# Low half of an expert's first weight matrix, moved from VectorE to GpSimd in a fused attention, FFN and mixture-of-experts kernel

## The chip, the cores and the metric

The kernel runs on one core of one Trainium2 chip. The metric is the device time of one execution in microseconds (us). A core has five engines that work at the same time and meet at semaphores: TensorE (PE: matrix products), VectorE (DVE), ScalarE (ACT), GpSimd (POOL) and SyncE (SP, which here only issues DMA transfers). Each takes its own instructions strictly in the order of the program.

## The reference

Four blocks act in turn on x of shape 16 x 128 x 256, each with a residual: cross attention with 16 heads; a gated FFN with fake quantisation; an mLSTM-like attention with 4 heads; and a mixture of 8 experts, of which every token uses 2. The change touches only the last:

```
logits = einsum('btd,de->bte', x, gate_w)
expert_weights, expert_indices = top_k(softmax(logits), 2)
expert_weights = expert_weights / expert_weights.sum(-1, keepdims=True)
for i in range(8):
    wi = where(expert_indices == i, expert_weights, 0).sum(-1)
    h = silu(x @ w1[i]) * (x @ w3[i])
    out = out + (h @ w2[i]) * wi[..., None]
```

w1 and w3 are 256 x 1024 for each expert, w2 is 1024 x 256.

## The kernel before, in words

The part around the change has two stages.

**Routing (about 357 to 385 us of the profiled execution).** VectorE works through one long chain of small instructions, lines 1820 to 1917. It picks each token's two experts (lines 1831 to 1842), counts the tokens of each expert (1849, 1850), lays the (token, expert) pairs into 39 tiles of 128 rows, all tiles of one expert side by side (1853 to 1887), and builds one-hot matrices (1891 to 1897) out of which TensorE makes the token number of every row (1033). `link_d` puts a wait behind nearly every one of these, so that each starts when the one before it has ended. Three results leave the chain. `tile_info` (lines 1870 to 1872, released by `info_ready` at 1874) holds the expert, the buffer and a flag "new expert" for each tile. The four one-hot pieces of line 1897 release TensorE's products of line 1033. `row_token` (line 1917, `info_ready` again) is what GpSimd needs for its gathers.

**Tiles (from about 385 us to the end).** For each of 39 tiles GpSimd gathers 128 token rows (`gather_rows`, line 667), TensorE transposes them (1059), ScalarE makes the bf16 high half of the transposed rows (`x_high`, 1333) and VectorE the low half (`x_low`, 1952); then come the products with w1 and w3 (`gate_up_half`, 1052), SiLU and product (1329, 1931), the transposes of the result (1065), its halves (1337, 1956), the product with w2 (1074), the weighting (1948) and the scatter-add by GpSimd (675).

All products of the experts are done as three bf16 products: high x high, high x low, low x high. So each weight matrix is stored twice, as a bf16 high half and a bf16 low half, which is the matrix minus its high half. `expert_w` has room for three experts; in it the high half of matrix n (0 is w1, 1 is w3, 2 is w2) is at n * PART and the low half at (3 + n) * PART. PART is 2048 elements in each of 128 partitions.

**The first expert** is known before the routing is, and is treated apart. SyncE loads its three matrices to `first_w` (line 463). ScalarE makes the high halves with `first_high` (1318): of matrices 0 and 1 before the pair weights, at 356.79 us for 3.70 us, of matrix 2 behind them. VectorE makes the low halves with `first_low` (lines 1919 to 1922): `first_low(0)` and `first_low(1)` behind `row_token` (1924, 1925), then, behind `x_low(0, 0)`, `first_low(2)` (1976). Who waits for these: TensorE for `part_low[0]` and `part_low[1]` before its first products of tile 0 (1050) and for `part_low[2]` before its first product with w2 (1070); ScalarE for all three at lines 1374 and 1375; SyncE for each before it loads that matrix for tile 2 (479).

**Later experts** are loaded to `stage`, and their halves made by `weights_high` on ScalarE (1346), by GpSimd for matrix 0 (`weights_low`, line 694) and by VectorE for matrices 1 and 2 (line 1911), only where the flag says that the tile has a new expert.

**GpSimd's order in the routing.** Constants (630 to 646), a gather that only warms up the queue (649), five small instructions for the pair weights (653 to 660, the second a power), and then nothing until `row_token` is there (wait at 678): then the gathers of tile 0 and tile 1 (680, 682), the wait at 698 and the loop over the tiles. SyncE stores the routed rows (`xrow_dram`, line 470) when line 660 has ended.

**TensorE's order** is the products of line 1033 in four groups of eight, then 40 products with no use but to keep the engine's clock up (`keep_clock(40, 0)`, lines 1096 and 714), then the transposes of tile 0 (1097) and `tile_step` 0.

Of the kernel before, what the change touches and what calls it, by code (L numbers as in the profile page):

```python
# [8 lines left out]
def build(nc, x, ctx_in, wq, wkv, wout, clip_x, clip_down, w_gate, w_up, w_down, ig_k, ig_b, fg_k, fg_b, rms_scale,  # L9
# [6 lines left out]
    ALU = mybir.AluOpType  # L16
# [13 lines left out]
    IR = I0 - (IT - 1) * P  # L30
    QMAX = 127.0
    E, _, F1 = w1.shape
    FH = F1 // 2
    TOP = 2
# [3 lines left out]
    PART = KT * F1  # L38
# [22 lines left out]
    with stack:  # L61
# [6 lines left out]
        def sem(name):  # L68
            return stack.enter_context(nc.semaphore(name))
# [102 lines left out]
        down_out = (down_even, down_odd)  # L172
        hT, x1n, xq = lay(region2, (F32, IT, B * P), (F32, B, D), (BF16, KT, B * P))
        _, hq = lay(region2, (F32, IT, B * P), (BF16, IT, B * P))


# [27 lines left out]
        expert_w = region2[:, :].bitcast(BF16)  # L204
        first_w = region2[:, SLOT // 2:SLOT].rearrange("p (n c) -> p n c", c=PART)
# [153 lines left out]
        part_high = [sem(f"part_high{i}") for i in range(3)]  # L359
        part_low = [sem(f"part_low{i}") for i in range(3)]  # L360
# [148 lines left out]
        def _(pool):  # L509
# [148 lines left out]
            pool.wait_ge(pair_weights, 4)  # L658
            nc.gpsimd.tensor_tensor(xrow[:, :, D + 2], w12[:, 0, :], w12[:, 1, :], ALU.subtract).then_inc(xrow_routed, 1)
            nc.gpsimd.tensor_tensor(xrow[:, :, D + 3], e2, w12[:, 0, :], ALU.mult).then_inc(xrow_routed, 1)  # L660

            def gather_rows(t):

                if t >= 2:
                    pool.wait_ge(tx_done, t - 1)
                    pool.wait_ge(meta_ready, t - 1)
                pool.indirect_dma_start(xg[:, t % 2, :], None, xrow_dram,  # L667
                                        bass.IndirectOffsetOnAxis(ap=row_token[:, t:t + 1], axis=0)).then_inc(xg_loaded[t % 2], 16)
# [716 lines left out]
        def _(dve):  # L1385
# [533 lines left out]
            def first_low(n):  # L1919
                dve.wait_ge(part_high[n], 1)  # L1920
                tt(expert_w[:, (3 + n) * PART:(4 + n) * PART], first_w[:, n, :], expert_w[:, n * PART:(n + 1) * PART],
                   ALU.subtract).then_inc(part_low[n], 1)

            first_low(0)
            first_low(1)
            info = [None, tile_values(1)]

# [74 lines left out]
```

## Time and profile before

| | us |
|---|---|
| median of 3 runs | 757.08 |
| lowest and highest of the 3 | 752.0, 757.09 |
| profiled execution | 756.54 |
| its span, from first to last instruction | 754.8 |
| outside the span (756.54 - 754.8) | 1.74 |

The profile is of one execution. A group of rows names engine, source line and shape; "x2" behind a row means that two instructions were merged, and its time is that of both. "Busy" counts the time in which an instruction of the engine is under way, and that includes time in which it is held up.

### The profile page before, as it was taken

To read this page: it belongs to the slowest core of one execution; us is meant where nothing else is said; L and a number is where in the kernel's file an instruction comes from. 1 tells how busy PE (TensorE), PEld (TensorE's weight loads), DVE (VectorE), ACT (ScalarE), POOL (GpSimd) and SP (SyncE) were. 2 spreads that over 40 slices of the span, in tenths; PEclk is the share of its full clock that TensorE was granted. 3 is DMA by queue.
4 is the path that set the end of the run, shared out by engine and by line. 5 is a ranking of instruction groups with operands and counts; after the bars stand their busy time and mean duration, and the time that the engine had idled before them with its cause. 6 is when DMAs were issued, how large, how long until landed. Compare 5 with 4: busy or idle time off the path is not lost.

```text
span 754.8 us, 17035 instructions
## 1 busy us (share of the span) xinstructions
PE 657.7 (87%) x4890; PEld 464.8 (62%) x4890; DVE 500.0 (66%) x1180; ACT 375.3 (50%) x878; POOL 291.9 (39%) x358
## 2 busy tenths in 40 slices
PE   2799999997777776898099999999999999999992
PEld 2588888886534545786056666666666666666661
DVE  6389899998588967797954746555464747554430
ACT  1366666665686643786223535363543635543320
POOL 3111111121153625577233736464553637543321
PEclk9799999999999999699589999999999999999996
DMA  8200000000300005336405253533415264421114
GB/s 282 47 15 14 14 14 14 14 0 1 112 0 1 0 1 172 128 82 226 135 23 174 49 150 76 150 85 84 140 31 153 73 181 126 116 43 29 31 15 125
DMA packets 47414, 59.01 MB, mean 78 GB/s; under 512 B 13328, under 2 KB 41168, under 8 KB 47056
## 3 DMA queue, kind: packets, MB, share of 16 engines
q1 hardware_dynamic: 39808, 47.72, 19.5%
q0 software_dynamic: 7536, 10.44, 7.8%
q8 instruction: 34, 0.56, 0.3%
q14 instruction: 36, 0.29, 0.1%
HBM read 145.96 MB, written 11.73 MB: 209 GB/s over the span
## 4 chain that ended last, share of the span: by engine, by line
PE 58%; DVE 20%; issue 8%; ACT 5%; DMA 2%; POOL 2%; DVEq 2%; ACTq 1%; SPq 0%; POOLq 0%
PE psum L1052 19%; PE psum L1074 11%; PE psum L752 5%; PE psum L1065 4%; PE psum L736 3%; PE psum L759 3%; PE psum L772 2%; ACT region L1346 2%; PE psum L791 1%; PE psum L741 1%; PE psum L714 1%; DVE region L1759 1%; DVE region L1777 1%; PE psum L779 1%; DVE region L1956 1%
## 5 line engine op out<-in xcount | busy, mean ns | idle before, releaser
L1052 PE MATMUL psum<-region 128*128 (+1 forms) x936 | 214.8, 379 | 1.6 <-DVE region L1952 1.6
L1052 PEld LDWEIGHTS psum<-region 128*128 128x128 bf16 x936 | 91.5, 98 | 95.5 <-DVE region L1952 1.2
L1329 ACT ACTIVATE region<-psum 128x512 f32<-128x512 f32 x78 | 46.5, 597 | 179.6 <-PE psum L1052 178.7
L675 POOL DMA_INDIRECT sum_dram<-region,row_token x39 | 75.2, 1927 | 135.3 <-DVE region L1948 135.3
L1074 PE MATMUL psum<-region 128*128 (+1 forms) x936 | 110.5, 275 | 5.3 <-DVE region L1956 5.3
L1074 PEld LDWEIGHTS psum<-region 128*128 128x128 bf16 x936 | 91.4, 99 | 18.9 <-issue 7.5
L1931 DVE TENSOR_TENSOR region<-psum,region 128x512 f32<-128x512 f32 x78 | 53.8, 690 | 68.3 <-ACT region L1329 68.3
L545 POOL TENSOR_TENSOR region<-region,pair_mask 128x256 f32<-128x256 f32 x32 | 21.3, 687 | 128.3 <-ACT region L1114 128.3
L1956 DVE TENSOR_TENSOR region<-psum,region 128x1024 bf16<-128x1024 f32 x39 | 47.6, 1221 | 17.7 <-ACT region L1337 17.5
L667 POOL DMA_INDIRECT region<-xrow_dram,row_token x39 | 41.4, 1062 | 38.0 <-DVE row_token L1917 13.6
L1421 DVE TENSOR_REDUCE region<-psum 128x8 f32<-128x1024 f32 x32 | 39.0, 1218 | 18.4 <-PE psum L752 18.4
L1948 DVE TENSOR_SCALAR region<-psum,region 128x256 f32<-128x256 f32 x39 | 18.8, 482 | 43.2 <-PE psum L1074 43.2
L1337 ACT ACTIVATE region<-psum 128x1024 bf16<-128x1024 f32 x39 | 39.9, 1023 | 13.4 <-PE psum L1065 13.4
L752 PE MATMUL psum<-region 32*128 32x256 f32 x256 | 38.1, 417 | 3.7 <-POOL region L545 3.6
L1118 ACT ACTIVATE region<-region 128x1024 f32<-128x1024 f32 x32 | 33.8, 1058 | 14.5 <-DVE region L1423 14.5
L1065 PEld LDWEIGHTS psum<-ident,region 128*128 128x128 f32 x312 | 36.5, 141 | 7.3
L714 PE MATMUL psum<-ident_b 128*128 128x256 bf16 x308 | 40.8, 288 | 0.0
L1065 PE MATMUL psum<-ident,region 128*128 128x128 f32 x312 | 40.4, 273 | 0.0
L1346 ACT ACTIVATE region<-region 128x2048 f32 x21 | 40.1, 1907 | 0.0
L1423 DVE TENSOR_TENSOR region<-psum,region 128x1024 f32<-128x1024 f32 x32 | 39.2, 1224 | 1.1
L1911 DVE TENSOR_TENSOR region<-region 128x2048 f32 x14 | 38.6, 2755 | 1.3 <-issue 1.3
L736 PE MATMUL psum<-region 128*128 128x128 f32 x256 | 34.4, 292 | 3.6 <-DMA region<-in_L_xattn_Wout 3.6
(298 smaller groups left out, 1220.3 us busy)
## 6 DMA issues: line engine op xcount, KB each, us to landing
region<-in_L_ffn_w SPq DMA_DIRECT2D x117, 1024.0 KB
region<-in_ctx SPq DMA_DIRECT2D x32, 128.0 KB, 2.4
xrow_dram<-region SPq DMA_DIRECT2D x1, 2080.0 KB, 7.8
x_sb<-in_x SPq DMA_DIRECT2D x4, 512.0 KB, 8.0
region<-in_ctx SPq DMA_DIRECT2D x2, 1024.0 KB, 7.0
region<-neg_max_dram SPq DMA_DIRECT2D x1, 2048.0 KB, 11.5
sum_dram<-x_sb SPq DMA_DIRECT2D x1, 2048.0 KB, 7.5
region<-neg_max_dram SPq DMA_DIRECT2D x4, 256.0 KB, 4.0
```

The lines of the kernel that those rows point to most:

```text
L667: pool.indirect_dma_start(xg[:, t % 2, :], None, xrow_dram, bass.IndirectOffsetOnAxis(ap=row_token[:, t:t + 1], axis=0)).then_inc(xg_loade ...
L675: pool.indirect_dma_start(sum_dram, bass.IndirectOffsetOnAxis(ap=row_token[:, t:t + 1], axis=0), y_d[:, t % 2, :], None, compute_op=ALU.ad ...
L714: mm(psum[:, bank_no, 0:256], ident_b[:], ident_b[:].unsqueeze(1).to_broadcast([P, 2, P]), start=True, stop=True)
L736: last = mm(bank1[:, m, :], w, xcT[:, p, (m // KT) * KT + k, :], start=(k == 0), stop=(k == KT - 1))
L752: last = mm(S_ps[s][:, 4 * r + 2 * m:4 * r + 2 * m + 2, :], qkT[rows, p, m, :], kbd[rows, p, m, :, :], start=True, stop=True)
L1052: last = mm(psum[:, 2 * f + n, :], (xT_lo if xl else xT_hi)[:, p, k, :], weights_at(place, wl, n, k * F1 + f * FH, FH), start=(i == 0), st ...
L1065: last = tr(bank(4, F1 // P, P, count=2)[:, f, :], h_d[:, p, f * P:(f + 1) * P], ident[:])
L1074: last = mm(psum[:, 7, 0:D], (hT_lo if hl else hT_hi)[:, f, :], weights_at(place, wl, 2, f * D, D), start=(i == 0), stop=(i == 3 * (F1 // ...
L1329: act_fn(sil_d[:, f, :], psum[:, 2 * f, :], ACT.Silu).then_inc(sil_d_ready, 1)
L1346: act_fn(expert_w[:, bass.ds(place + n * PART, PART)], stage[:, p, n, :], ACT.Copy)
L1931: tt(h_d[:, p, f * FH:(f + 1) * FH], psum[:, 2 * f + 1, :], sil_d[:, f, :], ALU.mult).then_inc(h_d_ready, 1)
L1956: tt(hT_lo, bank(4, F1 // P, P, count=2), hT_hi, ALU.subtract).then_inc(hT_low, 1)
```

## The change

GpSimd gets one instruction behind its pair weights: it waits for the high half of matrix 0 of the first expert, and subtracts it from that matrix. VectorE's call of `first_low(0)` behind `row_token` goes. Nothing else changes; the function `first_low` stays for matrices 1 and 2.

```diff
             nc.gpsimd.tensor_tensor(xrow[:, :, D + 2], w12[:, 0, :], w12[:, 1, :], ALU.subtract).then_inc(xrow_routed, 1)
             nc.gpsimd.tensor_tensor(xrow[:, :, D + 3], e2, w12[:, 0, :], ALU.mult).then_inc(xrow_routed, 1)
 
+            pool.wait_ge(part_high[0], 1)
+            nc.gpsimd.tensor_tensor(expert_w[:, 3 * PART:4 * PART], first_w[:, 0, :], expert_w[:, 0:PART], ALU.subtract).then_inc(part_low[0], 1)
+
             def gather_rows(t):
...
-            first_low(0)
             first_low(1)
             info = [None, tile_values(1)]
```

## Rows read from the trace of the kernel before

**Rows 1.** The page of the profile: busy shares (part 1) and the chain (part 4).
```profile
...
PE 657.7 (87%) x4890; PEld 464.8 (62%) x4890; DVE 500.0 (66%) x1180; ACT 375.3 (50%) x878; POOL 291.9 (39%) x358
...
PE 58%; DVE 20%; issue 8%; ACT 5%; DMA 2%; POOL 2%; DVEq 2%; ACTq 1%; SPq 0%; POOLq 0%
...
```

**Rows 2.** Chain that ended last, 350 to 430 us (start us, us, what).
```profile
...
373.02 4.55 DVE x_q L1897 x4
...
378.06 6.68 PE psum L714 x40
384.74 0.23 PE psum L1059 x2
385.00 0.39 ACT region L1333
...
385.83 2.21 DVE region L1921
...
```

**Rows 3.** Timeline of VectorE, 353 to 400 us; in brackets idle time and its releaser.
```profile
...
363.02 0.48 DVE L1858 TENSOR_TENSOR region<-region 128x312 f32<-128x312 f32 x1
...
365.43 0.20 DVE L1868 TENSOR_TENSOR region<-region 128x39 f32<-128x39 f32 x1
...
366.38 0.16 DVE L1875 TENSOR_TENSOR region<-region 128x8 f32<-128x8 f32 x1
...
378.39 0.20 DVE L1917 SCALAR_TENSOR_TENSOR row_token<-psum,row_empty 128x39 uint32<-128x39 f32 x1
378.51 4.48 DVE L1921 TENSOR_TENSOR region<-region 128x2048 bf16<-128x2048 f32 x2
385.41 0.42 DVE L1952 TENSOR_TENSOR region<-psum,region 128x256 bf16<-128x256 f32 x1 [2.42 <-ACT region L1333]
...
```

**Rows 4.** Timeline of GpSimd, 353 to 760 us.
```profile
...
361.56 2.94 POOL L655 TENSOR_TENSOR region<-region,minus_one 128x16 f32<-128x16 f32 x1
...
365.06 0.23 POOL L660 TENSOR_TENSOR region<-region 128x16 f32<-128x16 f32 x1
378.88 2.83 POOL L667 DMA_INDIRECT region<-xrow_dram,row_token  x1 [13.59 <-DVE row_token L1917]
382.02 1.81 POOL L667 DMA_INDIRECT region<-xrow_dram,row_token  x1 [0.30 <-issue]
...
416.93 3.81 POOL L694 TENSOR_TENSOR region<-region 128x2048 f32 x1
...
```

**Rows 5.** Line 667, the gathers: durations in ns, min/median/max, and to landing.
```profile
...
L667 POOL DMA_INDIRECT region<-xrow_dram,row_token x39: 940/997/2835, 378.9 to 710.6; - x39
...
DMA to landing us min/median/max: 2.6/2.9/5.5
```

**Rows 6.** SyncE's DMA queue, 360 to 400 us: waited in total, times, longest.
```profile
...
SPq L481 <- DVE region L1921: 10.0, 3, 5.7
...
```

**Rows 7.** Timeline of ScalarE, 353 to 400 us.
```profile
...
356.79 3.70 ACT L1318 ACTIVATE region<-region 128x2048 bf16<-128x2048 f32 x2
...
```

**Rows 8.** Timeline of VectorE, 412 to 432 us.
```profile
...
417.15 0.69 DVE L1931 TENSOR_TENSOR region<-psum,region 128x512 f32<-128x512 f32 x1 [1.31 <-ACT region L1329]
...
419.67 3.21 DVE L1911 TENSOR_TENSOR region<-region 128x2048 f32 x1 [0.18 <-issue]
...
428.88 2.29 DVE L1911 TENSOR_TENSOR region<-region 128x2048 f32 x1
...
```

**Rows 9.** Timeline of all engines, 287 to 291 us.
```profile
...
288.42 1.27 POOL L598 TENSOR_SCALAR_AFFINE_SELECT region<-region 128x512 f32<-128x512 f32 x2 [0.28 <-DVE region L1711]
...
289.23 0.73 DVE L1744 TENSOR_TENSOR_SCAN region<-ones_sb,region 64x128 f32<-64x128 f32 x1
...
290.31 0.42 DVE L1747 TENSOR_TENSOR_SCAN region<-ones_sb,region 64x128 f32<-64x128 f32 x1
...
```

**Rows 10.** TensorE by stretch: us, busy (instructions), granted clock, DMA share, GB/s.
```profile
...
361.00:374.00 13.00, 0.30 (x2) 0.50 0.49 164
...
382.00:383.00 1.00, 1.00 (x8) 0.67 0.45 133
...
```

## The prediction, made before the changed kernel was timed

> **What bounds the kernel now.** I read the page's shares first: TensorE is busy for 87% of the span, VectorE for 66%, GpSimd far less, and the chain that ended last is 58% TensorE and 20% VectorE [rows 1]. Such shares say nothing about one stage, so I next read the chain in order of time around the change. Through the routing it is VectorE's string of small instructions without a break, one row behind the other, up to the last one-hot piece (the four take 4.55 us from 373.02); then, behind the last products of line 1033, TensorE's 40 clock-keeping products (6.68 us) until 384.74, the transposes of tile 0, ScalarE's high half at 385.00, VectorE's `x_low` and, from 385.83, `first_low(2)` [rows 2]. The two `first_low` calls at 378.51 are not in it. Their row on VectorE's timeline is 4.48 us for both and ends at 382.99; the next one, `x_low` at 385.41, has 2.42 us of idle time before it, which ended with ScalarE's high half [rows 3]. So the removed instruction stands beside TensorE's 40 products, and what is added stands beside the one stretch in which VectorE alone sets the end. Third I read the timelines of the two engines where a long instruction of the one meets one of the other, since both will now be at work in that stretch.
>
> **What goes.** One 128x2048 subtraction on VectorE, 4.48 / 2 = 2.24 us [rows 3]. VectorE then has idle time from 380.75 instead of 382.99, and waits for the same high half: worth 0. Who else might gain? The first gather takes 2.83 us at 378.88 and the second 1.81 at 382.02, where the median one takes 1.0 [rows 4, 5]; they end 0.96 and 0.84 us behind the end of the first and of the second `first_low` (380.75 and 382.99). So each gather was held up by the subtraction beside it. But `first_low(1)` moves into the place of `first_low(0)`, so the first gather is held up as before; its rows land at the latest 378.88 + 5.5 = 384.38 [rows 4, 5], which TensorE, with its 40 products until 384.74, does not wait for. The second gather gets 0.8 us shorter, and its rows are wanted only behind the first products of tile 0. Worth 0. SyncE stood 10.0 us in three waits for the low halves [rows 6]; the first falls away, the last, for `first_low(2)`, stays where it is and brings SyncE to the same time. Worth 0. If I am wrong in all this and the whole instruction was on the path, the gain would be 2.24 us.
>
> **What is added on GpSimd.** The wait for `part_high[0]` is over long before: ScalarE made both first high halves from 356.79 us for 3.70 us [rows 7]. The instruction has the shape of line 694, 3.81 us [rows 4]. It starts behind line 660, 0.23 us from 365.06, so at about 365.3, and ends at 369.1. Behind it in GpSimd's queue are the gathers, which wait for `row_token` until 378.88 [rows 4]: 9.8 us of slack, cost 0. SyncE's store of the routed rows is released by line 660 and is not touched.
>
> **What it does to VectorE.** This is the term that decides. Look at the pair in tile 2's stretch: GpSimd's subtraction of line 694 starts at 416.93 and is nominally 3.81 us; VectorE's subtraction of line 1911, both inputs in SBUF, starts at 419.67 and takes 3.21 us; the same one, at 428.88 with no GpSimd arithmetic beside it, takes 2.29 [rows 4, 8]. It stood 0.92 us, until 420.59, which is 3.66 us behind the start of line 694. During the same line 694, VectorE's line 1931, one input from PSUM, takes 0.69 us [rows 8]. So the two engines exclude each other for whole instructions where VectorE has both inputs in SBUF; the long gathers above are the same with GpSimd as the one that stands. It holds for short ones too: the scan of line 1744, 64x128, takes 0.73 us beside GpSimd's line 598, and its like on line 1747 takes 0.42 [rows 9].
>
> From 365.43 on VectorE's chain has such instructions: line 1868 at 365.43 (two SBUF inputs, 128x39), the next at 366.38 (line 1875) [rows 3]. If GpSimd's starts at 365.3, line 1868 stands until 365.3 + 3.66 = 368.96, that is for 3.5 us. If line 1868 is first, GpSimd's starts some 0.3 us later and line 1875 is caught instead: 365.6 + 3.66 - 366.38 = 2.9 us. Bounds: from above the whole instruction, 3.8 us; from below 0, by the power of line 655, which took 2.94 us from 361.56 while line 1858 of VectorE, two SBUF inputs, took 0.48 for 312 elements, of which 0.34 is their share at `first_low`'s rate (2.24 us / 2048 = 1.1 ns each) [rows 3, 4], so it hardly stood. I take 3.5: the added instruction is a 2048-element subtraction like line 694, while the power has 16 elements and spends its time computing, not reading.
>
> All that follows is linked to it: the rest of the routing, the one-hot pieces, TensorE's products, the 40 products, the transposes [rows 2]. I find no slack in between: TensorE's groups of line 1033 wait for each one-hot piece. The 40 products begin at the granted clock 0.50 (1.2 GHz), at which TensorE stood from 361 us on; the stretch from 382 to 383, all busy, has the mean 0.67, so the clock rose to 1.00 (2.4 GHz) two thirds into it [rows 10]. I assume the same pattern, shifted. So +3.5 - 0 = +3.5 us.
>
> **A rule of the Trainium skill against the trace.** The rows of line 655 and of line 694 point in different directions. The Trainium skill, "SBUF — State Buffer", section "Who interferes with whom", says that a VectorE instruction with two SBUF inputs and a GpSimd one that reads SBUF share a port as an exclusive lock, held for the whole instruction by the one that issues first. The row of line 694 agrees (0.92 us of standing, to the end of the GpSimd instruction); that of line 655 does not, since line 1858 ran in the middle of it. By the rule the sum is +3.5 us, by the row of line 655 it is 0.
>
> **The sum.** Made against the profiled execution: 754.8 + 3.5 + 1.74 = 760.0 us. The median of the runs shown is 757.08, 0.5 above the profiled one, and one of the three runs is at 752.0, so a median may land some us off without any cause in the change; against the median the same term gives 760.6. The measurement tells about 1% (7.6 us) from no change, and 3.5 us is 0.5%.
>
> **The rivals.**
> - *Not slower: GpSimd's subtraction leaves VectorE's short instructions alone,* as the power did with line 1858. For it: that row. Against it: line 1744 was a short one and stood. VectorE then keeps its time and the removed 2.24 us are hidden: 756.5 us. It decides the case if the port is free between GpSimd's reads. Chance 0.13.
> - *Faster: the removed subtraction was on the path after all,* through the gather that it held up. It needs TensorE to wait for the gather, and the 40 products to end earlier than the gathered rows land; landing and end are only 384.74 - 384.38 = 0.36 us apart, but the first gather stays held up by `first_low(1)`. 756.5 - 2.2 = 754.3 us. Chance 0.05.
> - *Slower than forecast: the stall also costs clock.* In the trace the clock rose 4.8 us into the 40 products (they begin at about 378, it rises at about 382.7). If it rises only behind them, the 4.8 us at half speed and the 2.0 at full speed, until 384.74, become 4.8 + 2 x 2.0 = 8.8 us: 2.0 more, 762.0 us. For it: TensorE's feed of products is what stands still. Against it: the engine was at the low clock through the whole wait already [rows 10]. Chance 0.08.
> - The forecast, between +2.9 and +3.8: chance 0.74.
>
> **How the numbers follow.** The likeliest case is 760.0; on its own it spans 759.4 to 760.3, or 1 more by the median. The range takes in the case without a stall (756.5, with 1 below for the spread that the three runs show) and that of the late clock (762.0, with 1 above): 755.5 to 763.0. Only shifts as large as that of the run at 752.0 and the gain of 2.2 lie outside. All cases lie within 7.6 us: faster by over 1% 0.03, slower by over 1% 0.06, the rest 0.91.
>
> **What would show it.** In the new profile GpSimd has a 128x2048 instruction of about 3.8 us from about 365.3. Right: one VectorE row near 365.4 (line 1868; all lines below the added ones carry a number 3 higher) of about 3.7 instead of 0.20 us, `row_token` at about 382.0 instead of 378.39, the transposes of tile 0 at about 388.2, 2.42 + 2.24 = 4.7 us of idle time instead of 2.42 before `x_low`, the second gather about 1.0 us, and equal distances from tile to tile behind it. Wrong: if the row of line 1868 keeps 0.20 us, the lock is not held through such an instruction, and the first rival has it; if the stall is there but tile 0 starts at its old time, there was slack between 369 and 385 us that I did not see; if the 40 products take other than 6.8 us, the clock has its part.

## The result, and the profile after

| | before | changed |
|---|---|---|
| median of 12 runs | 756.44 | 760.46 |
| lowest and highest | 752.0, 759.23 | 758.27, 765.52 |
| span of the profiled execution | 754.8 | 757.4 |

The ratio of the two is given as 1.0066 (5.0 us), with a 95% interval of 1.0043 to 1.009: 3.3 to 6.8 us slower, 0.4 to 0.9 per cent. It is not the quotient of the two medians, which is 1.0053 (4.0 us). The forecast was +3.5 us and 760.0, near the lower end of the interval.

All lines below the added ones have a number 3 higher, and behind the removed call 2 higher: line 1868 of before is 1871, `first_low` is 1924, `x_low` 1954, `keep_clock` 717. The page first: its shares are those of before within a per cent [rows 1], and it would not lead anyone to the place.

```profile
...
PE 653.2 (86%) x4847; PEld 463.5 (61%) x4890; DVE 501.8 (66%) x1179; ACT 375.2 (50%) x878; POOL 295.1 (39%) x359
...
PE 57%; DVE 21%; issue 8%; ACT 5%; DMA 3%; POOL 2%; DVEq 2%; ACTq 1%; SPq 0%; POOLq 0%
...
```

VectorE's timeline, 355 to 402 us, against [rows 3]:

```profile
...
363.43 0.48 DVE L1861 TENSOR_TENSOR region<-region 128x312 f32<-128x312 f32 x1
...
365.85 3.93 DVE L1871 TENSOR_TENSOR region<-region 128x39 f32<-128x39 f32 x1
369.81 0.18 DVE L1872 TENSOR_SCALAR region<-region 128x39 f32<-128x39 f32 x1
...
382.54 0.20 DVE L1920 SCALAR_TENSOR_TENSOR row_token<-psum,row_empty 128x39 uint32<-128x39 f32 x1
382.65 2.28 DVE L1924 TENSOR_TENSOR region<-region 128x2048 bf16<-128x2048 f32 x1
389.05 0.42 DVE L1954 TENSOR_TENSOR region<-psum,region 128x256 bf16<-128x256 f32 x1 [4.11 <-ACT region L1336]
...
```

The instruction of line 1871, 128x39 elements, took 0.20 us before and takes 3.93 now. Everything else in the chain keeps its length: line 1861, beside the power, 0.48; the next one in line 0.18. `row_token` and the one remaining `first_low` follow, and VectorE's idle time before `x_low` grew from 2.42 to 4.11 us: the removed 2.24, less the half microsecond that TensorE's products became shorter (below). GpSimd's timeline, the same stretch, against [rows 4]:

```profile
...
365.47 0.23 POOL L660 TENSOR_TENSOR region<-region 128x16 f32<-128x16 f32 x1
365.65 4.07 POOL L663 TENSOR_TENSOR region<-region 128x2048 bf16<-128x2048 f32 x1
383.02 2.83 POOL L670 DMA_INDIRECT region<-xrow_dram,row_token  x1 [13.29 <-DVE row_token L1920]
386.16 0.96 POOL L670 DMA_INDIRECT region<-xrow_dram,row_token  x1 [0.30 <-issue]
...
```

The added instruction begins at 365.65 and ends at 369.72; line 1871 begins at 365.85 and ends at 369.78. The first gather still takes 2.83 us, the second fell from 1.81 to 0.96. The chain that ended last, against [rows 2], now goes through the stall:

```profile
...
365.85 3.94 DVE region L1871
...
377.16 4.55 DVE x_q L1900 x4
...
382.20 6.17 PE psum L717 x40
...
388.63 0.39 ACT region L1336
...
389.47 2.21 DVE region L1924
...
```

The chain's length is read from these rows of GpSimd and TensorE, before and after:

```profile
...
361.27 0.21 POOL L653 TENSOR_TENSOR region<-region,ones_sb 128x16 f32<-128x16 f32 x1 [3.62 <-ACT region L1323]
...
374.21 0.45 PE L1033 MATMUL psum<-region,x_q 128*128 128x39 f16 x8 [12.91 <-DVE x_q L1897]
...
377.90 6.84 PE L714 MATMUL psum<-ident_b 128*128 128x256 bf16 x40
384.58 0.38 PE L1059 MATMUL psum<-ident,region 128*128 128x128 f32 x2
...
```

```profile
...
361.68 0.21 POOL L653 TENSOR_TENSOR region<-region,ones_sb 128x16 f32<-128x16 f32 x1 [3.63 <-ACT region L1326]
...
378.35 0.45 PE L1036 MATMUL psum<-region,x_q 128*128 128x39 f16 x8 [16.65 <-DVE x_q L1900]
...
382.04 6.34 PE L717 MATMUL psum<-ident_b 128*128 128x256 bf16 x40
388.21 0.38 PE L1062 MATMUL psum<-ident,region 128*128 128x128 f32 x2
...
```

Of the 2.6 us between the two spans, this is where they arise. GpSimd's first pair-weight instruction (line 653) was 0.41 us later already (361.68 against 361.27), which is not the change's doing. The stall adds 3.93 - 0.20 = 3.73. The 40 clock-keeping products took 6.34 us on TensorE's timeline instead of 6.84, since this time the granted clock rose from 0.50 to 1.00 some 3.7 us into them and not 4.8: -0.50. So the transposes of tile 0 are 3.63 us later (388.21 against 384.58). At the scatters of tiles 0 to 11 it is 3.63 to 3.65; behind them it grows in small steps, whose cause was not looked for, to 4.09 at the last but one scatter (739.13 against 735.04); at the last it is 2.44 (745.27 against 742.83). There TensorE's last products with w2 took 2.82 us, where in the profile of before they took 4.46, at a mean granted clock of 0.61 instead of 1.00. This is the stretch 735 to 758 of the changed kernel (us, then busy time and instructions of PE, PEld, DVE, ACT and POOL, granted clock, DMA share, GB/s); the same stretch of before has a granted clock of 0.66:

```profile
...
735.00:758.00 23.00, 7.02 (x59) 5.36 (x57) 3.21 (x5) 1.62 (x2) 3.10 (x2) 0.77 0.35 103
...
```

A profile is one execution, and such differences of the clock come and go from one to the next: the last 24 products took 2.8 us in six of the thirteen profiles of this document and 4.3 to 4.5 in the other seven. So the 2.6 us between two single profiles is no measure of the change. What the medians' 4.0 us (or the ratio's 5.0) hold beyond the 3.73 of the stall is not traced; the interval begins at 3.3 us, so it may be nothing.

### The profile page after: what moved, and what is told of

It reads as the page before. It is cut to its first block, busy times and chain, and to the rows that moved or that the text cites. A ratio compares the mean times of both kernels' runs of the same rounds, so it can differ in the third digit from the quotient of the medians.

```text
span 757.4 us, 16992 instructions
## 1 busy us (share of the span) xinstructions
PE 653.2 (86%) x4847; PEld 463.5 (61%) x4890; DVE 501.8 (66%) x1179; ACT 375.2 (50%) x878; POOL 295.1 (39%) x359
## 4 chain that ended last, share of the span: by engine, by line
PE 57%; DVE 21%; issue 8%; ACT 5%; DMA 3%; POOL 2%; DVEq 2%; ACTq 1%; SPq 0%; POOLq 0%
PE psum L1055 19%; PE psum L1077 11%; PE psum L755 5%; PE psum L1068 4%; PE psum L739 3%; PE psum L762 3%; PE psum L775 2%; ACT region L1349 2%; PE psum L744 1%; PE psum L794 1%; DVE region L1762 1%; DVE region L1780 1%; PE psum L717 1%; PE psum L782 1%; DVE region L1958 1%
## 5 line engine op out<-in xcount | busy, mean ns | idle before, releaser
L1055 PE MATMUL psum<-region 128*128 (+1 forms) x897 | 206.5, 379 | 3.8 <-DVE region L1954 1.8
L1077 PE MATMUL psum<-region 128*128 (+1 forms) x936 | 109.3, 273 | 5.3 <-DVE region L1958 5.3
```

The costliest lines, as they stand in the source:

```text
L1055: last = mm(psum[:, 2 * f + n, :], (xT_lo if xl else xT_hi)[:, p, k, :], weights_at(place, wl, n, k * F1 + f * FH, FH), start=(i == 0), st ...
L1077: last = mm(psum[:, 7, 0:D], (hT_lo if hl else hT_hi)[:, f, :], weights_at(place, wl, 2, f * D, D), start=(i == 0), stop=(i == 3 * (F1 // ...
```

## The experiments

Theory 1 is the forecast: GpSimd's subtraction keeps one of VectorE's small instructions standing, and the removed one was beside the path. Theory 2: a part of the 4 us comes from what the removal does to the gathers or to SyncE. Theory 3: the removed instruction was on the path, and its gain was only outweighed. To be free of where a run stands when it comes to the routing, the chain's length is taken below from the start of GpSimd's first pair-weight instruction (line 653) to TensorE's first product of the one-hots (line 1033): 374.21 - 361.27 = 12.94 us before, 378.35 - 361.68 = 16.67 in the changed kernel. The kernel before was timed again beside the experiments: its median was 756.6 (35 runs) beside the removal alone, the addition alone, the 8 pieces and the subtraction behind the one-hots; 756.19 (17 runs) beside the writes only, the places behind the gathers and ahead of the pair weights, and the third low half; and 758.01 (a single run) beside the two versions without either subtraction and the change once more.

**The removal alone.** So that nobody waits for ever, ScalarE copies the matrix into the place of its low half; the values there are then not the low half.

```diff
+            act_fn(expert_w[:, 3 * PART:4 * PART], first_w[:, 0, :], ACT.Copy).then_inc(part_low[0], 1)
...
-            first_low(0)
             first_low(1)
```

> The removal alone: VectorE's first_low(0) goes, GpSimd gets nothing. So that part_low[0] is still released, ScalarE copies the matrix once more into the place of its low half (in its idle time behind first_high(2)); that part of the output's arithmetic is changed. Theory 1 (GpSimd's instruction stands VectorE up, the removed one was beside the path): the second gather falls from 1.8 to about 1.0 us, VectorE's idle time before x_low grows by 2.2 us, the transposes of tile 0 stay where they are counted from the first logits reduction, and the time is that of before within 0.3 us. Theory 2 (part of the change's 4 us comes from what the removal does to the gathers or to SyncE): the time differs from before by a us or more. Theory 3 (the removed instruction was on the path and its gain was only outweighed): 2.2 us faster than before.

Measured: median 756.18 of 12 runs, ratio to before 0.9989 (0.9966 to 1.0012). The chain is 371.50 - 358.57 = 12.93 us long. GpSimd's two gathers:

```profile
...
376.17 2.83 POOL L667 DMA_INDIRECT region<-xrow_dram,row_token  x1 [13.57 <-DVE row_token L1918]
379.31 0.96 POOL L667 DMA_INDIRECT region<-xrow_dram,row_token  x1 [0.30 <-issue]
...
```

The second has fallen to 0.96, the first still takes 2.83, and neither makes anything start earlier. Theory 3's 2.2 us would be a ratio of 0.997, which the interval just holds, but the profile speaks against it: VectorE's idle time before `x_low` has grown from 2.42 to 3.67 us (not by the 2.2 expected, since the 40 products were 0.97 us shorter here) and again ends with ScalarE's high half, so the removed work had been done while VectorE had nothing else.

**The addition alone.** VectorE keeps both calls, GpSimd's result goes where nobody reads it.

```diff
+            pool.wait_ge(part_high[0], 1)
+            nc.gpsimd.tensor_tensor(expert_w[:, 17 * PART:18 * PART], first_w[:, 0, :], expert_w[:, 0:PART], ALU.subtract)
```

> The addition alone: GpSimd does the same 128x2048 subtraction at the same place, but into a part of expert_w that nobody reads yet, and VectorE keeps both first_low calls. Theory 1: VectorE's fourth-last slot instruction (two SBUF inputs, 128x39) stands for 3.7 us, the transposes of tile 0 come 3.2 to 3.7 us later, and the time is that of the changed kernel, some 3 to 4 us over before. Theory 2 or 3: since nothing is removed, the time would be below the changed kernel's by what the removal costs, or 2.2 us above it.

(Meant is line 1868, as in the prediction.) Measured: median 759.59 of 12 runs, ratio 1.0041 (1.0019 to 1.0063); chain 375.22 - 358.55 = 16.67 us, to the hundredth that of the changed kernel. VectorE's timeline, and the second gather on GpSimd's, which is long again because `first_low` is back beside it:

```profile
...
362.71 3.93 DVE L1871 TENSOR_TENSOR region<-region 128x39 f32<-128x39 f32 x1
...
```

```profile
...
383.02 1.81 POOL L670 DMA_INDIRECT region<-xrow_dram,row_token  x1 [0.30 <-issue]
...
```

So the addition alone makes the stall, and the removal adds nothing to it that a timing resolves.

**The same work in 8 pieces.**

```diff
-            nc.gpsimd.tensor_tensor(expert_w[:, 3 * PART:4 * PART], first_w[:, 0, :], expert_w[:, 0:PART], ALU.subtract).then_inc(part_low[0], 1)
+            for c in range(8):
+                at = c * PART // 8
+                last = nc.gpsimd.tensor_tensor(expert_w[:, 3 * PART + at:3 * PART + at + PART // 8], first_w[:, 0, at:at + PART // 8], expert_w[:, at:at + PART // 8], ALU.subtract)
+            last.then_inc(part_low[0], 1)
```

> The changed kernel with GpSimd's subtraction cut into 8 pieces of 256 elements in a row. Theory 1 with the port held for one instruction and no longer: VectorE's row of 3.93 us goes, and several of its rows with two SBUF inputs stand for at most 0.5 us each instead; their sum is less than 3.7 us, because the rows with one input run on meanwhile: about 1.5 to 2.5 us in all. Rival (the port goes back to VectorE only when GpSimd's queue of such instructions is empty): one stall of 3.7 us or more, as before. Rival (no exclusion, but a slower GpSimd start or the like): the number of pieces changes nothing.

VectorE's timeline shows seven short stalls for the one long (lines are 3 further down again; 1874 is the instruction that was 1871):

```profile
...
365.75 0.55 DVE L1874 TENSOR_TENSOR region<-region 128x39 f32<-128x39 f32 x1
366.33 0.58 DVE L1875 TENSOR_SCALAR region<-region 128x39 f32<-128x39 f32 x1
366.94 0.59 DVE L1876 CAST tile_info<-region 128x39 int32<-128x39 f32 x1
...
367.54 0.65 DVE L1878 CAST tile_info<-region 128x39 int32<-128x39 f32 x1
368.23 0.59 DVE L1880 TENSOR_SCALAR region<-region 128x39 f32<-128x39 f32 x1
...
368.92 0.53 DVE L1882 TENSOR_SCALAR region<-region 128x8 f32<-128x8 f32 x1
369.48 0.79 DVE L1883 TENSOR_TENSOR region<-region 128x128 f32<-128x128 f32 x1
...
```

Over the lengths of before (0.17 to 0.37) that is 2.8 us, and the chain is 377.37 - 361.58 = 15.79 long, 2.85 more than before. GpSimd's eight pieces:

```profile
...
365.56 5.25 POOL L665 TENSOR_TENSOR region<-region 128x256 bf16<-128x256 f32 x8
...
```

So the turn goes from one engine to the other between instructions, not only when GpSimd is done with all of them; GpSimd's eight together took 5.25 us, against 4.07 in one piece. How much of the difference is giving way, and how much the start of eight instructions, was not tried. My expectation was wrong in one point, and so in the sum (1.5 to 2.5 us): lines 1875, 1876, 1878, 1880 and 1882 (1869, 1870, 1872, 1874 and 1876 of before) have one input each, and stood as well. The median is 758.72 of 10 runs, 2.1 us over that of before; the ratio is 1.0012 (0.9992 to 1.0033), that is 0.9 us and at most 2.5, less than the chain's 2.85. In this profile the 40 products took 7.30 us; how much of a stall they take up on average was not tried.

**Writes only.** The removal alone (with ScalarE's copy, which the lines below leave out), and in the place of GpSimd's subtraction a fill.

```diff
+            nc.gpsimd.memset(expert_w[:, 17 * PART:18 * PART], 0.0)
```

> The removal alone, and in GpSimd's place of the added subtraction a fill with zeros of 128x2048 bf16, which writes and reads nothing (into a part of expert_w that nobody reads yet; the first low half is again a copy made by ScalarE, so that part of the arithmetic is changed). Theory 1a (VectorE's second SBUF input and GpSimd's reads exclude each other): the 128x39 instruction with two inputs keeps its 0.20 us beside the fill. Theory 1b (any GpSimd access of that length excludes any of VectorE's): it, or the one-input instruction beside it, stands until the fill's end, for 1 to 2 us.

VectorE's timeline and, below it, GpSimd's:

```profile
...
364.11 0.18 DVE L1869 TENSOR_SCALAR region<-region 128x39 f32<-128x39 f32 x1
364.32 1.85 DVE L1870 TENSOR_SCALAR region<-region 128x39 f32<-128x39 f32 x1
366.21 0.20 DVE L1871 TENSOR_TENSOR region<-region 128x39 f32<-128x39 f32 x1
...
```

```profile
...
364.34 1.80 POOL L662 MEMSET region<- 128x2048 bf16 x1
...
```

Theory 1b, in a narrower form. The fill ran for 1.80 us from 364.34, and the instruction that was then to start, line 1870 (1867 of before), one input and a scalar, stood 1.67 us. The chain is 374.99 - 360.38 = 14.61 us long, the same 1.67 more than before. The one with two inputs came behind the fill's end, so this run does not tell whether it would have stood. In this profile a GpSimd instruction that reads nothing was enough to stop a one-input float32 instruction of VectorE. The single run took 755.66, which says nothing about 1.67 us.

**Other places for GpSimd's subtraction.** First, behind the last one-hot piece:

```diff
+            pool.wait_ge(hot_ready, 4)
             pool.wait_ge(part_high[0], 1)
```

> The changed kernel, but GpSimd waits for the last one-hot piece before its subtraction, so that it begins when VectorE's chain of routing is over (at about 377.6 us of the time before). Theory 1: the 3.93 us row falls back to 0.20 and the one-hot pieces come as early as in the kernel before; in exchange first_low(1) stands for some 2.9 us, and the first gather, behind the subtraction in GpSimd's queue and then behind first_low(1), ends some 4.5 us later than before, its rows land at about 387 to 389, and tile 0 begins 2.5 to 4.5 us late: no better than the changed kernel. Rival (the stall has no part in the 4 us): tile 0 is later than in the changed kernel by all of this.

```profile
...
378.00 5.34 DVE L1925 TENSOR_TENSOR region<-region 128x2048 bf16<-128x2048 f32 x1
...
```

```profile
...
386.11 0.44 PE L1063 MATMUL psum<-ident,region 128*128 128x128 f32 x2 [1.60 <-DMA region<-xrow_dram,row_token]
...
```

The chain is back at 12.94 us (373.71 - 360.77). `first_low(1)` took 5.34 us, 3.06 of them standing; the first gather came behind GpSimd's subtraction, at 381.36, and took 2.91; TensorE waited 1.60 us for the gathered rows when its 40 products were done. Tile 0's transposes began 386.11 - 377.11 = 9.00 us behind the start of the last group of line 1033, against 6.96 before: 2.0 us late, less than the 2.5 to 4.5 expected. Median 759.58 of 10 runs, ratio 1.0034 (1.0017 to 1.0052): the price is paid at another place, and the timings do not show it to be smaller.

Second, behind the gathers of tiles 0 and 1 (the two added lines below `gather_rows(1)`):

> The changed kernel with GpSimd's subtraction behind the gathers of tiles 0 and 1, so beside nothing of VectorE's chain. Theory 1: no row of 3.9 us on VectorE, the transposes of tile 0 as early as in the kernel before, x_low unharmed (one of its inputs is in PSUM), but TensorE's first product waits for part_low[0], which comes at about (end of the second gather) + 4 us: tile 0 starts some 1 to 2 us late, and first_low(2), two SBUF inputs, stands until the subtraction's end.

TensorE's timeline and VectorE's:

```profile
...
387.63 2.75 PE L1055 MATMUL psum<-region 128*128 128x512 bf16 x12 [1.89 <-POOL region L685]
...
```

```profile
...
386.19 0.42 DVE L1954 TENSOR_TENSOR region<-psum,region 128x256 bf16<-128x256 f32 x1 [4.98 <-ACT region L1336]
386.54 3.11 DVE L1924 TENSOR_TENSOR region<-region 128x2048 bf16<-128x2048 f32 x1
...
```

Much as expected: chain 12.94, `x_low` unharmed at 0.42 beside GpSimd's subtraction, `first_low(2)` with 0.83 us of standing, and TensorE idle for 1.89 us before tile 0's first product, instead of 0.93 before, so 0.96 late by that (1 to 2 us were expected). A single run took 758.03.

Third, ahead of the pair weights:

> The changed kernel with GpSimd's subtraction ahead of the pair weights, as early as ScalarE's high half allows (about 2.6 us before the place of the change). Theory 1: the stall moves with it: another of VectorE's instructions with two SBUF inputs, of 128x128, stands for 3.4 to 3.9 us, the time is the changed kernel's. Rival (only the place behind line 660 is bad): no stall of that size.

```profile
...
358.61 0.29 DVE L1834 TENSOR_REDUCE region<-region 128x16 f32<-128x128 f32 x1
358.93 3.72 DVE L1835 TENSOR_TENSOR region<-region 128x128 f32<-128x128 f32 x1
...
```

```profile
...
358.45 4.05 POOL L653 TENSOR_TENSOR region<-region 128x2048 bf16<-128x2048 f32 x1 [1.12 <-ACT region L1321]
...
```

The stall moved to line 1835 (1832 of before), 128x128 elements, 3.72 us instead of 0.29. The reduction just ahead of it, one input of 128x128, began 0.16 us into GpSimd's subtraction and kept its 0.29 us. So not every one-input instruction of VectorE stands: in these profiles `tensor_scalar` and casts stood, a reduction did not. Here the chain is counted from VectorE's first reduction, since line 653 comes behind the subtraction: 377.30 - 356.67 = 20.63 us, against 374.21 - 357.00 = 17.21 before: 3.4 more. A single run took 760.08.

**What VectorE's subtractions do to the first gather, and what hides it.** Both calls go, ScalarE copies both matrices into the places of their low halves; then the same with 24 products instead of 40.

```diff
-            keep_clock(40, 0)
+            keep_clock(24, 0)
```

> VectorE's first_low(0) and first_low(1) both go (ScalarE copies the two matrices into the places of their low halves, so that part of the arithmetic is changed), GpSimd gets nothing. If VectorE's subtraction is what holds up the first gather, its 2.83 us fall to about 1.0 us and its rows land some 1.9 us earlier after row_token; with its 40 products TensorE still begins tile 0 at the end of those, so the time is that of before. If the first gather is long for a reason of its own, it keeps 2.8 us.

> The same with 24 instead of 40 clock-keeping products. If the first gather was held up by VectorE and the 40 products hid that, tile 0's transposes now start 1.0 to 2.0 us earlier after the last one-hot piece than in the kernel before (6.96 us there); if not, they wait for the gathered rows and gain at most 0.3 us.

GpSimd's first gather in the former, and TensorE's products and first transposes in the latter:

```profile
...
378.84 1.04 POOL L667 DMA_INDIRECT region<-xrow_dram,row_token  x1 [13.60 <-DVE row_token L1919]
...
```

```profile
...
378.39 5.07 PE L714 MATMUL psum<-ident_b 128*128 128x256 bf16 x24
383.29 0.38 PE L1059 MATMUL psum<-ident,region 128*128 128x128 f32 x2
...
```

The first gather takes 1.04 us instead of 2.83, so it was VectorE's subtraction that held it up. With 40 products tile 0 begins where it did (384.64 - 377.58 = 7.06 us behind the start of the last group of line 1033, against 6.96 before). With 24 it begins 383.29 - 378.11 = 5.18 us behind it, 1.8 us earlier. A single run each took 756.96 and 754.1, against 758.01 for the kernel before. That the 40 products also hide the slow gather in the kernel before is argued, not shown: the version with 24 products and both subtractions on VectorE was not run. Nor can 24 be trusted to keep the clock: here the granted clock rose at 383.1 us, 0.2 us ahead of the transposes and 4.7 into the 5.07 us of the products, while in the profile of the 8 pieces it rose 5.7 us into them.

**A use for VectorE's idle time without GpSimd.** The kernel before, with its third low half ahead of `x_low`.

```diff
             first_low(0)
             first_low(1)
+            first_low(2)
...
             x_low(0, 0)
-            first_low(2)
```

> The kernel before, with first_low(2) moved ahead of x_low(0, 0) into the 2.42 us in which VectorE stood idle; nothing goes to GpSimd. Theory 1 (that idle time is free): x_low starts within 0.1 us of its old distance from the transposes, ScalarE's wait for the three low halves is over as soon as it comes to it, and the 0.64 us in which TensorE stood before the first product of tile 1 goes: 0.3 to 0.7 us faster than before, 3.5 to 5 faster than the changed kernel. Rival: the first or second gather is held up longer and delays tile 0: no gain.

```profile
...
386.49 2.76 PE L1052 MATMUL psum<-region 128*128 128x512 bf16 x12 [0.93 <-DVE region L1953]
...
389.31 5.34 PE L1052 MATMUL psum<-region 128*128 128x512 bf16 x24
...
```

TensorE's two halves of 12 products, of tile 0 and tile 1, now stand as one row of 24 without the 0.64 us between them. From the transposes of tile 0 to the first scatter it is 401.76 - 385.18 = 16.58 us, against 401.97 - 384.58 = 17.39 before, and the 0.81 us are still there at the last but one scatter (349.65 against 350.46 us behind the same transposes). So the idle time was free, as theory 1 has it, and using it was worth 0.8 us (0.3 to 0.7 were expected), not the 2.2 us of the instruction that was moved. The timing can't show it: median 756.51 of 12 runs, ratio 1.0014 (0.9985 to 1.0044). That a version with this and without the first gather's delay would beat the kernel before is argued from this run and the two above, not shown; none with the full arithmetic was run.

**The change once more.**

> The changed kernel itself, a second profile. The row of 3.93 us on VectorE and that of 4.07 us on GpSimd come again within 0.05 us; the 40 clock-keeping products, 6.34 us in the first profile of it and 6.84 in that of the kernel before, may take another time, between 5.8 and 7.4 us, since they did so from run to run.

```profile
...
369.55 3.94 DVE L1871 TENSOR_TENSOR region<-region 128x39 f32<-128x39 f32 x1
...
```

3.94 us, with GpSimd's at 4.07 again, in an execution that took 764.77 us; most of its length arose ahead of the routing, whose first reduction began at 361.10 instead of 357.39. The chain from there is 382.07 - 361.10 = 20.97 us, in the first profile 378.35 - 357.39 = 20.96. The 40 products took 6.73 us, inside the 5.8 to 7.4 expected. The stall is the same in both, and the spread of the times comes from elsewhere.

## Why the prediction was right

- *What goes is worth 0.* Right: the chain without the removed instruction is 12.93 us against 12.94, and the time the same within its interval. That the first gather would stay held up by `first_low(1)`, and the second get 0.8 shorter, came as written (2.83 and 0.96).
- *What is added costs nothing on GpSimd itself.* Right: it ended at 369.7, the first gather began at 383.02. It was mis-sized a little: 4.05 to 4.07 us in each run that has it in one piece, not the 3.81 of line 694.
- *The deciding term: line 1868 stands.* Right, at the place named: 3.73 us instead of 3.5. The difference is about that by which GpSimd's instruction is longer (0.26).
- *The lower bound 0, by the power.* Did not apply, as reasoned: beside the power VectorE's 128x312 instruction took 0.48 us again, in the same profile in which the subtraction stopped one of 128x39 for 3.7.
- *No slack between the chain and tile 0.* Right with a reserve. In the profile 3.63 of 3.73 + 0.41 arrived, since the 40 products were half a microsecond shorter; for the same reason the idle time before `x_low` was 4.11 us and not the 4.7 forecast. The clock did not cost more in this execution, as the third rival had it, but less. Over the profiles the stall has no price in clock that shows: the 40 products took 5.89 to 6.79 us in the four with the stall in one piece, and 5.87 to 7.20 in the six with no stall in the chain.
- *Luck.* The transposes of tile 0 were forecast for about 388.2 and began at 388.21. That it fits so closely is chance: a stall 0.23 us longer and a start 0.41 us later met products 0.50 us shorter. The median of 760.46 lies 0.5 us from the forecast of 760.0, but the medians and the ratio differ by a microsecond, so the timing confirms the direction and the rough size, and it is the profiles that confirm the term.
- *The rule of the Trainium skill* on the shared port ("SBUF — State Buffer", "Who interferes with whom") gave the same sum, and the runs agree with it in this: stalls end with the other engine's instruction, and each engine's turn lasts for an instruction (8 pieces, seven stalls). They do not agree that every GpSimd instruction keeps the port for its whole length: the power, 2.94 us, left line 1861 its 0.48. Why it differs stays open: that it computes more than it reads was the prediction's argument, and no run varied it.
- Where I was too narrow: I looked only for VectorE instructions with two SBUF inputs. Those with one input stood too, in the 8 pieces and beside the fill, though not the reduction beside the subtraction. It made no difference to the sum, because the first to be caught was line 1868, with two.

## What to carry to other kernels

Idle time on an engine is no reason to give it work: ask what the other one is doing in that stretch, since here GpSimd's subtraction and VectorE's instructions stopped each other for up to a whole instruction, and one of 128x39 in a linked chain paid for one of 128x2048 beside it (3.73 of its 4.07 us). Look for a pair of rows in the trace in which the two already meet; one such pair gave the stall here to a quarter of a microsecond. And before moving work off an engine, read what ended its next idle time: if it is not that engine, the move is worth nothing.

## What the runs showed of the hardware that I had not expected

- A GpSimd fill that reads nothing stopped a float32 instruction of VectorE with one input and 39 elements for 1.67 us. A reduction of VectorE with one input of 128 elements was not stopped by GpSimd's subtraction (0.29 us).
- GpSimd's power of 16 elements, 2.94 us long, stopped nothing; its subtraction of 2048 elements stopped the first two-input instruction of VectorE that came, at both places in the chain.
- GpSimd's indirect gather is stopped by VectorE's subtraction (2.83 us, and 1.04 without it).
- The same 40 products behind the same chain took from 5.87 (the removal alone) to 7.30 us (8 pieces), by where in them the clock rose from 1.2 to 2.4 GHz (2.8 and 5.7 us into them); the last 24 products of the kernel took 2.8 us in some profiles and 4.3 to 4.5 in others, in the same way (mean granted clock 1.00 in the changed kernel's, 0.61 in that of before). Single profiles differ by one or two microseconds for that alone, up to about half of what this change is worth.
